# Norm folded into per-image stem weights in five sets; low weight parts by accumulating transfers; idle products on TensorE

## What is computed

```python
x_aux = _cbs(x, w_sta, b_sta)          # 1x1 conv 256 -> 128, bias, silu: the "stem"
y1, y2 = [x_aux], [x_aux]
for _ in range(3):
    y1.append(_tmaxavg(y1[-1]))        # 0.9 * 5x5 max + 0.1 * 5x5 mean
    y2.append(_rwpool(y2[-1]))         # sumpool(e * x) / (sumpool(e) + 1e-06), e = exp(x - max(x))
...
x = x + _L0_conv_ref(_gn(x), ...)
x = x + _L1_conv_ref(_gn(x), L1_conv_w1, L1_conv_w2)
```

## Time and profile before

| | us |
|---|---|
| median of three runs | 1413.25 |
| lowest and highest | 1409.47, 1413.27 |
| the profiled execution | 1411.98 |
| its span in the profile | 1410.2 |
| stem, to the barrier | 88.7 |
| level loop, to the barrier | about 173 |
| rest | about 1148 |

### The profile page before, as it was taken

One profiled execution on the slowest core, in us unless ns is written; L12 is line 12 of the kernel. 1 busy time (PEld: TensorE's weight loads), 2 busy tenths in 40 slices (PEclk: granted clock), 3 DMA queues, 4 the chain that ended last, 5 costly groups with the idle time before them and its releaser, 6 DMA issues.

```text
span 1410.2 us, 18374 instructions
## 1 busy us (share of the span) xinstructions
PE 1278.9 (91%) x7162; PEld 1067.5 (76%) x7162; DVE 1149.0 (81%) x1217; ACT 704.2 (50%) x762; POOL 159.5 (11%) x76
## 2 busy tenths in 40 slices
PE   3569899859999999999999999999999999999697
PEld 1249898647689868986898689868986888688597
DVE  7779897898898879887998799879887988785443
ACT  0246768554465356535653654365436553654342
POOL 1557668200000000000000000000000000000000
PEclk9779999879999999999999999999999999999899
DMA  7302213110000200020002000200020002001000
GB/s 295 149 30 81 85 75 118 62 60 30 15 1 16 90 15 0 15 89 15 0 15 89 15 0 15 89 15 0 15 89 15 0 30 75 0 1 60 0 1 30
DMA packets 19319, 63.37 MB, mean 45 GB/s; under 512 B 1616, under 2 KB 4304, under 8 KB 19280
## 3 DMA queue, kind: packets, MB, share of 16 engines
q1 hardware_dynamic: 18576, 62.53, 11.9%
q10 hardware_dynamic: 704, 0.30, 0.1%
HBM read 37.13 MB, written 25.17 MB: 44 GB/s over the span
## 4 chain that ended last, share of the span: by engine, by line
PE 53%; issue 13%; DVE 11%; ACT 4%; DVEq 0%; ACTq 0%; POOLq 0%; POOL 0%
PE slot L1140 19%; PE slot L1178 13%; PE ps_level L1178 9%; DVE between L1459 4%; PE slot L1194 3%; PE slot L553 3%; PE slot L1118 2%; DVE a L1459 2%; PE slot L1165 1%; PE ps_level L1210 1%; ACT f_all L1329 1%; PE slot L1097 1%; ACT a L1362 1%; ACT f_all L1365 1%; DVE f_all L1486 1%
## 5 line engine op out<-in xcount | busy, mean ns | idle before, releaser
L1178 PE MATMUL slot<-f_all,q_all 128*128 128x512 f32 x768 | 197.1, 409 | 13.4 <-ACT pooled L1319 13.4
L1178 PE MATMUL ps_level<-v_all,pt_all 128*128 128x256 f32 x1536 | 200.0, 287 | 5.4 <-ACT mixed L1338 5.2
L1178 PEld LDWEIGHTS ps_level<-v_all,pt_all 128*128 128x128 f32 x1536 | 189.6, 192 | 7.7 <-DVE pt_all L1463 6.2
L1178 PEld LDWEIGHTS slot<-f_all,q_all 128*128 128x128 f32 x768 | 145.2, 195 | 44.0 <-ACT pooled L1319 14.8
L1459 DVE SCALAR_TENSOR_TENSOR a<-between,k_columns,a 128x992 f32<-128x992 f32 (+1 forms) x128 | 157.5, 1231 | 4.9 <-ACT a L1310 2.6
L1059 POOL TENSOR_TENSOR c_rstd<-c_spread,k_minus_half 128x2 f32<-128x2 f32 x8 | 5.6, 698 | 1065.9 <-DVE gmean L1531 1065.9
L1463 DVE TENSOR_TENSOR pt_all<-slot,pt_all 128x1024 fp32r<-128x1024 f32 x64 | 78.2, 1221 | 48.2 <-ACT pt_all L1324 48.2
L1118 PE MATMUL slot<-wide,k_cv 128*128 128x512 f32 x256 | 114.3, 597 | 0.0
L1333 ACT CAST v_all<-y 128x1024 fp32r<-128x1024 f32 x32 | 33.7, 1053 | 159.5 <-DVE y L1490 159.4
L1338 ACT ACTIVATE mixed<-ps_level,row_inv 128x256 f32<-128x256 f32 x64 | 30.2, 471 | 152.6 <-PE ps_level L1178 152.6
L1310 ACT ACTIVATE a<-between,k_columns 128x1024 f32<-128x1024 f32 x64 | 79.5, 1242 | 50.1 <-DVE between L1459 49.2
(11 more groups left out here) (179 smaller groups left out, 2730.4 us busy)
## 6 DMA issues: line engine op xcount, KB each, us to landing
levels<-x_all SPq DMA_DIRECT2D x32, 512.0 KB, 2.6
x_all<-in_x SPq DMA_DIRECT2D x8, 1024.0 KB, 13.3
q_all<-levels SPq DMA_DIRECT2D x8, 1024.0 KB, 4.9
x<-in_x SPq DMA_DIRECT2D x8, 1024.0 KB, 4.8
out<-x SPq DMA_DIRECT2D x8, 1024.0 KB, 3.9
pooled<-levels SPq DMA_DIRECT2D x8, 512.0 KB, 3.4
wide<-levels SPq DMA_DIRECT2D x7, 512.0 KB, 3.3
x_all<-in_w_c SPq DMA_DIRECT2D x2, 512.0 KB, 3.9
```

The lines of the kernel that those rows point to most:

```text
L1178: last = nc.tensor.matmul(out, lhs, rhs, start=(n == 0), stop=(n == len(parts) - 1))
```

## The change

- **Norm in the weights.** `xn` and `normalise` are gone. ACT makes for each image `w_image = w_sta * rstd` (two 128 x 128 instructions, `weigh`), PE multiplies `w_sta` by `shift` (`biases`), ACT adds the bias to that (`b_image`), and `convolve` reads the raw image.
- **Five sets.** The chain of statistics runs for the images (0), (1), (2, 3), (4, 5), (6, 7), and its products stand between halves of the convolutions.
- **Weights.** They are loaded into tiles of their own right behind the images. ACT writes the high part and its negative (`minus_hi`); a DMA from POOL's queue adds the negative into the raw tile (`accum_op`), and ACT copies the sum into the low tile: cv2 in the stem, the other four in steps 2 to 5 of the level loop. POOL waits for all five transfers at the end of the stem. The last two steps of level 0 of the chain and its mixture move from the stem to step 0 of the loop, and all of levels 1 and 2 one step later; so does `WHOLE`.
- **Idle products.** `keep_warm` multiplies the identity by itself into a PSUM tile that is not read: 6 times before the first group sums, 12 at the end of the stem, 8 and 4 at the start of the loop.
- **DVE in the loop.** In step 0 the last maxima and the mixture of level 0 stand between the second `product` and the first `residual`; the step of level 1 behind the first `divide` has left for step 1.
- **Borders.** `turn(0)` stands ahead of `spread_max(0)`; at a new level `reduce_batch` stands ahead of `product` on DVE and `set_eps` and `estimate` ahead of `product_hi` on ACT. The first level copy for the box sums reads `x_all` instead of a transferred copy.

```diff
-STAGED = {"w1": (0, 1, 0, 512), "w2": (0, 1, 512, 1024), "cvend": (1, 2, 0, 1024), "c1": (2, 4, 0, 1024), "cv2": (4, 5, 0, 1024)}
+SETS = ((0,), (1,), (2, 3), (4, 5), (6, 7))
+WEIGHTS = ("cv2", "c1", "cvend", "w1", "w2")
+SET_OF = {n: g for g, images in enumerate(SETS) for n in images}
...
+            for k in WEIGHTS:
+                raw = raw_weights[k].rearrange("p (t o) -> p t o", o=SPLIT[k][1])
+                sp.dma_start(raw, rows(k)).then_inc(weights_in[k], 16)
...
-            for k in SPLIT:
-                sp.wait_ge(xn_done, STAGED[k][1] * CT)
-                n = STAGED[k][1] - STAGED[k][0]
-                for j in range(n):
-                    sp.dma_start(raw[k][:, j].rearrange("p (t o) -> p t o", o=SPLIT[k][1]),
-                                 w[k].rearrange("(n t p) o -> n p t o", p=P, n=n)[j]).then_inc(weights_in[k], 16)
...
+            def weigh(g):
+                act.wait_ge(rstd_done, g + 2)
+                for n in SETS[g]:
+                    for t in range(CT):
+                        at = n * CT + t
+                        nc.scalar.activation(w_image[:, n, t], w_sta[:, t], ACT.Copy, scale=rstd[:, at:at + 1]).then_inc(weighted_done, 1)
+                act.wait_ge(bias_sum_done, g + 1)
+                part = images_of(g)
+                nc.scalar.activation(b_image[:, part], ps_bias[:, part], ACT.Identity, bias=keep["b_sta"]).then_inc(bias_done, 1)
...
             def split(k):
-                act.wait_ge(weights_in[k], 16 * (STAGED[k][1] - STAGED[k][0]))
-                nc.scalar.copy(flat(keep[k + "_hi"], k), raw[k]).then_inc(split_done, 1)
-            for n in range(3):
-                silu(n)
+                act.wait_ge(weights_in[k], 16)
+                raw = raw_weights[k]
+                nc.scalar.copy(flat(k), raw).then_inc(hi_done, 1)
+                nc.scalar.mul(minus_hi[k], raw, -1.0).then_inc(minus_done, 1)
...
+            weigh(0)
+            silu(0)
+            weigh(1)
+            act.wait_ge(stem_done, 3)
             act.wait_ge(chain.borders, chain.n_borders)
-            chain.zero_first(act)
+            chain.zero_first(image2d(x_all[:, 0, 0]))
+            silu(1)
+            weigh(2)
+            silu(2)
+            weigh(3)
             silu(3)
+            split("cv2")
+            split("c1")
+            silu(4)
+            weigh(4)
+            split("cvend")
+            silu(5)
+            split("w1")
+            split("w2")
+            silu(6)
+            act.wait_ge(low_in["cv2"], 16)
+            nc.scalar.copy(keep["cv2_lo"][:, :, :].rearrange("p t o -> p (t o)"), raw_cv2[:, :]).then_inc(pooled.weights_low, 1)
+            silu(7)
+            act.wait_ge(box_in, 16)
+            nc.scalar.copy(box[:, :], box_raw[:, :]).then_inc(box_ready, 1)
             act.wait_ge(cv1_in, 16)
...
-            split("w1")
-            split("w2")
-            silu(4)
-            split("cvend")
-            silu(5)
-            split("c1")
-            silu(6)
-            split("cv2")
-            silu(7)
-            act.wait_ge(box_in, 16)
-            nc.scalar.copy(box[:, :], box_raw[:, :]).then_inc(box_ready, 1)
-            chain.zero_next(act, 1)
...
+            def biases(g):
+                pe.wait_ge(shift_done, g + 1)
...
+                for k in range(CT):
+                    last = nc.tensor.matmul(ps_bias[:, images_of(g)], w_sta[:, k, :],
+                                            shift[:, SETS[g][0] * CT + k:last_of(g) * CT:CT],
+                                            start=(k == 0), stop=(k == CT - 1))
+                last.then_inc(bias_sum_done, 1)
+            def convolve(n, h):
+                if h == 0:
+                    pe.wait_ge(weighted_done, CT * n + CT)
+                    pe.wait_ge(stem_done, n + 1)
+                for k in range(CT):
+                    last = nc.tensor.matmul(ps[:, n % 2, h * HALF:(h + 1) * HALF], w_image[:, n, k],
+                                            x_all[:, n, k, h * HALF:(h + 1) * HALF], start=(k == 0), stop=(k == CT - 1))
...
-            statistics(0)
-            for n in range(group - 1):
-                convolve(n, n % 2)
-            statistics(1)
-            convolve(group - 1, (group - 1) % 2)
-            with pe.Fori(group // 2, B // 2) as pair:
-                for u in range(2):
-                    convolve(pair * 2 + u, u)
+            keep_warm(nc, keep, ps_warm[:, 0:P], 6)
+            means(0)
+            variances(0)
+            biases(0)
+            convolve(0, 0)
+            means(1)
+            convolve(0, 1)
+            variances(1)
+            biases(1)
+            convolve(1, 0)
+            convolve(1, 1)
+            means(2)
+            variances(2)
+            biases(2)
+            for g in range(2, len(SETS)):
+                first, second = SETS[g]
+                convolve(first, 0)
+                convolve(first, 1)
+                if g + 1 < len(SETS):
+                    means(g + 1)
+                convolve(second, 0)
+                if g + 1 < len(SETS):
+                    variances(g + 1)
+                convolve(second, 1)
+                if g + 1 < len(SETS):
+                    biases(g + 1)
+            keep_warm(nc, keep, ps_warm[:, 0:P], 12)
...
-            chain.box_sums(pool, 0, 0)
-            low_parts(("w1", "w2"))
-            low_parts(("cvend", "c1", "cv2"))
+            box_sum_steps(0)
+            inverse_deviations(2)
+            box_sum_steps(1, 2)
+            inverse_deviations(3)
+            box_sum_steps(3, 4)
+            inverse_deviations(4)
+            box_sum_steps(5)
+            for n, k in enumerate(WEIGHTS):
+                pool.wait_ge(hi_done, n + 1)
+                pool.wait_ge(minus_done, n + 1)
+                pool.dma_start(raw_weights[k], minus_hi[k].bitcast(F32),
+                               accum_op=ALU.add).then_inc(low_in[k], 16)
+            for k in WEIGHTS:
+                pool.wait_ge(low_in[k], 16)
...
-            def normalise(n):
-                u = n % 2
-                dve.wait_ge(sta_done, n + 1)
-                for t in range(CT):
-                    at = n * CT + t
-                    nc.vector.tensor_scalar(xn[:, u, t], x_all[:, n, t], rstd[:, at:at + 1], shift[:, at:at + 1],
-                                            ALU.mult, ALU.add).then_inc(xn_done, 1)
...
-            for i in range(group):
-                take_stats(i)
+            take_stats(0)
+            aggregate(0)
             deviations(0)
-            take_stats(group)
+            take_stats(1, 0)
+            add_eps(0)
+            take_stats(1, 1)
             shifts(0)
-            normalise(0)
-            normalise(1)
-            for i in range(group + 1, B):
-                take_stats(i)
-                if i - group + 1 < group:
-                    normalise(i - group + 1)
+            take_stats(1, 2, 3)
+            aggregate(1)
+            take_stats(2, 0)
             deviations(1)
+            take_stats(2, 1, 2)
+            add_eps(1)
+            take_stats(2, 3)
...
-            for n in range(group + 1, B):
-                normalise(n)
-                maximum(n - 3)
-                chain.maxima(dve, 0, 0, *between[n - group - 1])
-            maximum(B - 3)
-            chain.mixture_of_sums(dve, 0)
-            maximum(B - 2)
-            maximum(B - 1)
+            add_eps(3)
+            take_stats(6, 0)
+            shifts(3)
+            take_stats(6, 1, 2, 3)
+            take_stats(7)
+            aggregate(4)
+            maximum(2)
+            deviations(4)
+            maximum(3)
+            add_eps(4)
+            chain.maxima(dve, 0, 0, 0)
+            shifts(4)
+            maximum(4)
+            chain.maxima(dve, 0, 0, 1, 2)
+            maximum(5)
+            chain.maxima(dve, 0, 0, 3)
+            maximum(6)
+            chain.maxima(dve, 0, 0, 4)
+            maximum(7)
...
+def keep_warm(nc, keep, out, times):
+    for _ in range(times):
+        nc.tensor.matmul(out, keep["ident"][:, :], keep["ident"][:, :], start=True, stop=True)
...
-WHOLE = frozenset([*range(1, 7), *range(11, 17)])
...
+WHOLE = frozenset([*range(2, 8), *range(12, 18)])
...
+                    sp.wait_ge(pooled.weights_low, len(WEIGHTS))
...
+            turn(0)
             spread_max(0)
+            keep_warm(nc, keep, ps_ey[:, 0:P], 8)
             for s in range(-2, total):
                 if s and level_starts(s):
                     spread_max(s // B)
                 if s >= 0:
                     sum_ey(s)
-                if s + 2 < total:
+                if s == -1:
+                    turn(1)
+                    keep_warm(nc, keep, ps_ey[:, 0:P], 4)
+                elif 0 <= s and s + 2 < total:
                     turn(s + 2)
...
+                if first and s:
+                    set_eps(s // B)
+                if s >= 0 and (s or not first):
                     estimate(s)
```

(31 more changed lines are left out.)

132 lines of the change are left out of this document (77 added, 55 removed).

## The result

The changed kernel took 1419.03 us (median of 6 runs, 1417.2 to 1422.1), the kernel before 1412.67 beside it: ratio 1.0051, 95% interval 1.0034 to 1.0067. It is slower by half a per cent, where the prediction had 1389.5 and a range that ended at 1404. The profiled execution of the changed kernel took 1421.92 us (span 1420.1), that of before 1411.98 (span 1410.2), so there are 10 us to explain on the profiles, and 34 us against the 1388.1 that the sum gave for a profiled execution.

A forecast was written before the change was run, and what follows sets the result against it. The stem was taken as bound first by waiting for four images' statistics, then by DVE, its gain passed on whole. Stem -21.0, loop -2.9 and block 3 0 took 1413.25 to 1389.5 us; range 1380 to 1404.

The forecast's parts named there:

- the load near 68: Sign at the stem's end: ScalarE's table load, which opens the level loop, comes near 68 us, against 88.69 before.
- The chain of sets: Stem, statistics through convolutions of the five sets: first silu at 25 us instead of 30.6, fourth near 44.5.
- Rival 1: Stem: the chain of small steps becomes the bound, costing 7 us more, stem end at 74, time 1396.5; chance 0.15.
- ScalarE's tail and DVE: Stem behind the fourth silu: ACT's queue is the bound, 20.3 us until 64.8; DVE ends with it, `normalise` gone.
- The transfers: Stem's end: five accumulating transfers, 2.6 MB, issued at 55; bounds 64 and 69, taken as landing at 67.
- The loop: Level loop: terms -1.0 + 0.5 - 2.0 + 2.2 - 2.6 sum to -2.9 us, bounds -7 and +2.
- Step 0: Loop's first step: two maxima and a mixture on DVE, about 1.2 us each, 3.6 in all, partly in idle time: +0.5.
- Low parts: Loop, ACT's copies of low parts: +1.4 us for c1, +0.6 for cvend, +0.2 for w1 and w2.
- Borders: Loop, starts of new levels: reduction and estimate moved ahead bring the estimate about 1.3 us earlier, twice: -2.6.
- The chains one step later: Loop: chain work leaving step 0 and `WHOLE` moving from step 1 to 7 save some -2 us early, part given back.
- Rival 4: Idle products lift nothing: slow 6.48 us convolutions in the first sets, some 4 us, 1393.5; chance 0.62 together with the forecast.
- Slower: Outcome slower than before: transfers at some tenth of the copy rate end at 120 us, time 1442; chance 0.05.

The follow-up runs named there:

- e1: The changed kernel with the five accumulating transfers as plain copies, so low parts are not computed: 1406.26 us.
- e7: The changed kernel with the level stores of images 4 to 7 held until the accumulating transfers of w1 and w2 land: 1414.99 us.
- e3: The changed kernel with the last two maxima and the mixture of level 0 back at the end of DVE's stem: 1409.20 us.
- e2: The changed kernel without ACT's four low-part copies in the loop; POOL zeroes those low parts at the stem's start: 1409.95 us.
- e4: The kernel before with one added 1.89 us ScalarE copy of c1's high part onto itself at step 2: 1420.66 us.
- e10: e5 with only the borders' reordering added (reduce_batch ahead of product, set_eps and estimate ahead of product_hi): 1402.64 us.
- e6: The changed stem with low parts by subtraction, and the changed loop without its copies, step 0 cleared as in e3: 1401.82 us.
- e5: The changed stem with low parts by subtraction on GpSimd and VectorE, and the loop of the kernel before: 1394.02 us.
- e8: The changed kernel without its idle products: 1416.24 us.
- e11: e9 with 8 more idle products behind c1's landing and the changed kernel's start of the loop: 1390.48 us, ratio 0.9836 to 0.9875.
- e9: e5 with c1 and cvend by accumulating transfer and a copy each, and no idle products ahead of the first set: 1393.34 us.

## Why the prediction was wrong

**Its conditions for being wrong did not come, and it was wrong.** They were transfers landing after 75 (74.4) and block 3 moving by more than 2 us (0.6); no DVE instruction over 1.3 us between 45 and 65 was right as well. They watch the stem and block 3, where the smaller part of the miss lies. Of the signs that it named, the load near 68 (75.5), the landing by 69 (74.4) and the first residual 12 us behind the loop's start (17.8) failed.

**The chain of sets: right.** First silu forecast at 25, came at 24.33; fourth at 44.5, came at 43.38. Rival 1 (five rounds of small steps as the bound) didn't come about.

**ScalarE's tail and DVE: right.** ScalarE ended at 62.15, forecast 64.8; the 16 `normalise` and their waits were gone.

**The transfers: the term was mis-sized, by 7.4 us.** The step that failed was "I take 67, between the two", and before it the upper bound of 69. The rate of the upper bound, 12.8 us for the bytes, was close to the 13.75 measured (e1: half of a copy's). What the bound left out is what else was in the queue: four level stores of 2.10 MB in the same stretch, 4.4 us by e7. These stores are in the kernel before, and the sentence "then little is moved" looked only at the totals. An estimate of the upper bound from the same rows is 55 + 12.8 + 2.10 MB at 410 GB/s (5.1) + a start, 74; that it comes so close to 74.4 is partly luck, since the last issue stood at 58.5.

**The loop: the mechanism was missing.** This is the larger part, 25.4 of the 33.8 us, about 22 without the step 20 of this one execution. The step that failed is "about 1.2 each by the reduction of as many columns": a reduction has one input in SBUF, the maxima and the mixture have two, and GpSimd's subtractions run beside them. The prediction priced each instruction in the loop at its own length. It had a row of the effect: `normalise` beside GpSimd at 2841 ns, and drew from it only that those rows go away. The trace of before even has the two maxima in question, at the stem's end beside a subtraction of GpSimd:

```profile
76.08 4.41 DVE L228 TENSOR_TENSOR work_b<-work_a 128x1024 f32<-128x1024 f32 x1
...
80.52 3.24 DVE L228 TENSOR_TENSOR work_b<-work_b,tall 128x1024 f32<-128x1024 f32 x1
```

What failed, term by term:

- Step 0, "+0.5" for two maxima and a mixture: 5.2 us up to y(0) and 3.2 more in step 1 (e3). They were priced at 1.2 each; two stand beside GpSimd's `e_lo` and `ey_lo` and last 3.3 and 3.2, the other 2.2.
- Low parts, "+2.2": 8.2 us from y(0) to y(8) (e2). The copies hold the steps' phase so that `e_lo` starts before the maximum. e4 shows the mechanism free of everything else: 1.9 us added, 6.1 us paid in the five steps behind it.
- Borders, "-2.6": the wait went as computed, 3.35 to 1.47, but the reordering alone makes the loop 5.6 us longer (e10), since what follows collides.
- The chains one step later, priced at 0 but for "some -2 early on": the first steps are shorter (5.7, 6.2 in e6 against 6.7, 6.6 in e5), though e6 also has the idle products and turn 0 ahead. With the border's reordering it ends in a loop 4.3 us longer than the old one (e6 against e5), with step 18 at 9.3 instead of 5.4. e10, with the chains in place, loses 5.6, so the reordering costs without the shift; the shift alone has no run.
- Slow products behind the gaps belong to these terms: behind 6.56 and 3.10 us of idle TensorE ran at half its rate. How long it stays slow differs between executions; in step 20 of this profile it made 3.2 us.

Without step 20's 3.2 us, e2 and e3 each shorten the loop by 8.7 us, and both together (e6, 177.1) by 15.9, a little under their sum. With the old loop it is 172.8.

**Block 3: right**, 0.6 us off. It came out at 1145.2 to 1145.8 in three runs and 1147.7 to 1148.4 in the others; comparisons under 3 us in the medians above carry that uncertainty, and what sets it stays open.

**Rival 4** (idle products that lift nothing) was half right: the six ahead of the first set are a cost (2.3 us between e8 and the changed kernel, less in other executions); those at the loop's start help once the collisions of step 0 are gone.

**Slower** was given 0.05 and tied to one cause, transfers at a tenth of a copy's rate. The slowness came from the loop, where every edit had been costed with the neighbours' timing held fixed.

What remains open: how often a given order of `e_lo` and the maxima would stay flipped for other delays (e4 tried one), what part of the loss in step 18 itself belongs to the clock and what to the collision (only step 20's part is told apart), and what makes the slow stretches of the clock end sooner in one execution than in another.

## What to carry to other kernels

In a software pipeline whose engines start within tenths of a microsecond of each other, an inserted instruction isn't priced by its length: look up what starts within its length on VectorE and GpSimd, and whether VectorE's instruction has two inputs in SBUF or one, since here the later of the two waited for the whole of the other and the order stayed flipped for up to four steps. Take the price of an instruction from a row with the same inputs. Price a transfer with everything that is in flight beside it, stores that were there before included, and ask which barrier waits for its issuer. When a change moves several things, run each block old and new crosswise: here the new stem with the old loop was worth 1.1%, and e11, built from it, 1.45%, while the whole change lost 0.5%.

## What the runs showed of the hardware

- An accumulating transfer inside SBUF took 2.05 times the DMA engines' time of a plain one with the same bytes: 13.75 against 6.7 us for 2.62 MB.
- One 1.89 us copy on ScalarE made the five steps behind it 6.1 us longer; three maxima that had started ahead of GpSimd's subtraction started behind it (e4). A two-input maximum of 1.22 us took 3.3 us with GpSimd 0.1 us ahead of it and up to 4.42 beside a longer subtraction (e5); a reduction with one input kept its 1.21.
- In the changed kernel TensorE's last products of the stem ended at 62.4; its granted clock was 1.00 until 66 and 0.50 from 68 on (2.4 and 1.2 GHz), and groups of ten products took 2.33 us instead of 1.31. In e9 the granted clock was still 0.50 in the windows up to 84, 16 us behind the first product of the loop, with TensorE nearly always busy from 74 on; in e11, kept busy from 68, it was 1.00 from 74.
- Executions of the same instructions differ in when the granted clock comes back: behind the gap of step 18 at 1.00 from 240 in e7 (10 us behind the maximum) and from 252 in the changed kernel (17 behind), worth 3.2 us in step 20.
